# Unread products on TensorE ahead of a gather, one expert slot's products ahead of the fill tables, and scatters ahead of gathers on GpSimd

## What is computed

```python
probs = jax.nn.softmax(logits, axis=-1)
_, idx = jax.lax.top_k(probs, TOPK)
weights = probs * jax.nn.one_hot(idx, E, dtype=probs.dtype).sum(-2)
out = jnp.zeros_like(x)
for e in range(E):
    h = jax.nn.silu(x @ w1[e]) * (x @ w3[e])
    out = out + h @ w2[e] * weights[:, e:e + 1]
x = x + jnp.tanh(g_ffn[0]) * out
```

## Time and profile before

| | us |
|---|---|
| median of three runs | 699.2 |
| lowest and highest run | 697.81, 699.62 |
| profiled execution | 698.2 |
| its span, first to last instruction | 696.4 |
| TensorE busy | 638.3 (92%) |
| VectorE busy | 600.1 (86%) |
| ScalarE busy | 549.8 (79%) |
| GpSimd busy | 463.8 (67%) |

### The profile page before, as it was taken

One profiled execution on the slowest core, in us unless ns is written; L12 is line 12 of the kernel. 1 busy time (PEld: TensorE's weight loads), 2 busy tenths in 40 slices (PEclk: granted clock), 3 DMA queues, 4 the chain that ended last, 5 costly groups with the idle time before them and its releaser, 6 DMA issues. The chain is left out here.

```text
span 696.4 us, 14843 instructions
## 1 busy us (share of the span) xinstructions
PE 638.3 (92%) x4509; PEld 584.2 (84%) x4510; DVE 600.1 (86%) x1386; ACT 549.8 (79%) x1927; POOL 463.8 (67%) x646
## 2 busy tenths in 40 slices
PE   1579999999999999999999999999998479999994
PEld 0578899999999999999999999999977457888883
DVE  7797899999989999998999999888898877777771
ACT  5787889998998999999899999988875245666670
POOL 4777777688677768867786886787565425454532
PEclk9989999999999999999999999999999669999998
DMA  7101100020020102002000110200099412323232
GB/s 224 61 1 57 36 1 31 2 61 32 1 62 2 32 1 62 32 1 62 1 32 1 54 42 2 62 2 1 1 355 341 159 31 49 52 53 53 46 45 23
DMA packets 35509, 37.72 MB, mean 54 GB/s; under 512 B 2704, under 2 KB 30352, under 8 KB 35440
## 3 DMA queue, kind: packets, MB, share of 16 engines
q1 hardware_dynamic: 31024, 30.84, 13.3%
q0 software_dynamic: 4416, 6.03, 5.4%
HBM read 31.62 MB, written 5.24 MB: 53 GB/s over the span
## 5 line engine op out<-in xcount | busy, mean ns | idle before, releaser
L1459 POOL TENSOR_SCALAR shared<-shared,rsum 128x256 f32<-128x256 f32 x256 | 143.8, 573 | 56.1 <-DVE rsum L1004 51.0
L707 ACT ACTIVATE shared<-s,nmax 128x256 f32<-128x256 f32 x256 | 122.2, 498 | 22.9 <-DVE nmax L999 22.7
L1453 POOL TENSOR_TENSOR rstd<-rstd,half 128x7 f32<-128x7 f32 (+1 forms) x64 | 88.8, 1387 | 5.3
L999 DVE TENSOR_REDUCE nmax<-s 128x2 f32<-128x512 f32 x128 | 86.7, 680 | 3.1 <-PE s L380 3.0
L1009 DVE TENSOR_TENSOR pt_lo<-t,pt_hi 128x512 fp32r<-128x512 f32 x124 | 84.2, 679 | 1.9 <-ACT pt_hi L715 0.9
L715 ACT CAST pt_hi<-t 128x512 fp32r<-128x512 f32 x124 | 74.1, 597 | 9.8 <-PE t L395 7.2
L723 ACT ACTIVATE shared<-route_bank,head_w 128x512 f32<-128x512 f32 (+1 forms) x124 | 81.5, 689 | 0.0
L395 PE MATMUL t<-ident,shared 128*128 128x128 f32 x496 | 75.3, 275 | 5.9 <-POOL shared L1459 2.7
L994 DVE TENSOR_TENSOR qk_lo<-shared,qk_hi 128x512 fp32r<-128x512 f32 x96 | 78.3, 815 | 2.4 <-POOL qk_hi L1470 1.3
L336 PE MATMUL pj_a<-w_ring,xq 128*128 128x256 f32 x488 | 72.9, 293 | 6.9 <-POOL xq L1535 6.9
L2007 DVE TENSOR_TENSOR w_lo<-expert_w,w_hi 128x1024 fp32r<-128x1024 f32 x46 | 56.2, 1224 | 25.6 <-ACT w_hi L1885 24.9
(11 more groups left out here) (275 smaller groups left out, 1929.1 us busy)
## 6 DMA issues: line engine op xcount, KB each, us to landing
expert_w<-in_w SPq DMA_DIRECT2D x24, 512.0 KB, 9.2
spare<-in_wT SPq DMA_DIRECT2D x19, 256.0 KB, 3.1
wp_raw<-in_wpT SPq DMA_DIRECT2D x16, 256.0 KB, 2.9
spare<-in_wkvT SPq DMA_DIRECT2D x16, 128.0 KB, 3.3
spare<-in_wT SPq DMA_DIRECT2D x9, 128.0 KB, 3.6
spare<-in_x SPq DMA_DIRECT2D x1, 1024.0 KB, 5.9
x_hat<-acc SPq DMA_DIRECT2D x1, 1024.0 KB, 4.6
out<-spare SPq DMA_DIRECT2D x1, 1024.0 KB, 6.9
```

Of the source, the lines that this page charges most:

```text
L707: e = act.activation(probs[:, st, h * S:(h + 1) * S], s_bank[st][:, h * S:(h + 1) * S], ACT.Exp, bias=nmax[:, st, h:h + 1], accum_out=psum ...
L999: dve.tensor_reduce(nmax[:, st, :], s_bank[st][:].rearrange("p (h t) -> p h t", h=2), AX, ALU.max, negate=True).then_inc(max_done, 1)
L1453: pool.tensor_tensor(rstd[:, st, c], rstd[:, st, c], half[:, c], ALU.pow).then_inc(rstd_ready, 1)
L1459: m = pool.tensor_scalar(probs[:, st, c], probs[:, st, c], rsum[:, st, h:h + 1], 1.0, ALU.mult, ALU.mult)
```

## The change

Five edits in `experts`:

1. TensorE multiplies the identity by 128 columns of `acc` ten times ahead of its wait for `slots_known`, and twice more behind the transposes of slot 0. The products go to a bank that is written anew before it is read.
2. On TensorE the fill products go behind `down(0)`; `down(1)`, which writes over them, waits for `out_known`.
3. On VectorE the register load of slot 0's expert comes first, then the four operations up to `factor`, then the weight remainders of slot 0, then four of the operations that split `factor`, then the row split of slot 0 and `last_rows`, then the last of the nine.
4. On VectorE `take_hidden(0)` and the copy to `row_scale` come ahead of the fill tables, and `out_rows_known` goes into step 0, ahead of `take_y(0)`.
5. On GpSimd five gathers go ahead of the wait for `out_known` instead of four, and then scatter n goes ahead of gather n + 5.

```diff
@@ tensor
+            def stay_awake(times):
+                for _ in range(times):
+                    pe.matmul(h3_bank[1][:, 0:P], ident[:], acc[:, 0, 0:P], start=True, stop=True)
+
+            stay_awake(10)
             pe.wait_ge(slots_known, 1)
             turn_rows(0, 0)
+            stay_awake(2)
             hidden(0, 0, 0)
...
                 if isinstance(n, int) and n == 0:
-                    find_fill()
                     pe.wait_ge(scales_known, 1)
                     pe.wait_ge(tokens_known, 1)
+                if isinstance(n, int) and n == 1:
+                    pe.wait_ge(out_known, 1)
                 down(n, par)
+                if isinstance(n, int) and n == 0:
+                    find_fill()
@@ vector
-            (L1972 to L1984, the nine linked operations, ahead of the rest)
...
+                if isinstance(n, int) and n == 0:
+                    out_rows_known()
+                    dve.wait_ge(scales_known, 1)
                 take_y(n, par)
...
             e = expert_of(0)
+            (wait for exped and f_gated, L1974 to L1977)
             weights_rest(0, 0, e, 0)
             weights_rest(0, 0, e, 1)
+            (L1979 to L1983)
             rows_rest(0, 0)
             last_rows()
+            (L1984)
             slot_scales()
             e = expert_of(1)
             weights_rest(1, 1, e, 0)
             rows_rest(1, 1)
             weights_rest(1, 1, e, 1)
+            take_hidden(0, 0)
+            dve.wait_ge(scales_found, 1)
+            dve.tensor_copy(row_scale[:], y_bank[0][:, 0:SLOTS]).then_inc(scales_known, 1)
             fill_places()
             fill_table()
-            dve.wait_ge(scales_found, 1)
-            dve.tensor_copy(row_scale[:], y_bank[0][:, 0:SLOTS]).then_inc(scales_known, 1)
-            take_hidden(0, 0)
-            out_rows_known()
-            dve.wait_ge(scales_known, 1)
             steps(dve, step)
@@ gpsimd
-            for n in range(4):
+            for n in range(5):
                 load(n, n % 2)
             pool.wait_ge(route.sums_begun, 16)
             pool.wait_ge(out_known, 1)
             for n in range(SLOTS):
-                if n + 4 < SLOTS:
-                    load(n + 4, n % 2)
-                if n >= 1:
-                    scatter(n - 1, (n - 1) % 2)
-            scatter(SLOTS - 1, (SLOTS - 1) % 2)
+                scatter(n, n % 2)
+                if n + 5 < SLOTS:
+                    load(n + 5, (n + 1) % 2)
```

More of the change, by code:

```diff
@@ L1737, in experts @@
             sem("last_known"), sem("last_ranked"), sem("fill_known"), sem("fill_found"), sem("out_known"))
+        factored = sem("factored")
         weighed, scales_found, scales_known = sem("weighed"), sem("scales_found"), sem("scales_known")
@@ L1970, in _ @@
             dve.tensor_scalar(slot_expert[:], slot_f[:], float(E - 1), None, ALU.min).then_inc(slots_known, 1)
[L1972 to L1984, removed]
             def slot_scales():
@@ L2075, in _ @@
             e = expert_of(0)
+            dve.wait_ge(exped, 1)
+            dve.wait_ge(route.f_gated, 1)
+            link(dve.tensor_reduce(total[:], prob[:, :, 0:E], AX, ALU.add))
+            link(dve.reciprocal(total[:], total[:]))
+            link(dve.tensor_scalar(total[:], total[:], route.fgate[:, 0:1], None, ALU.mult))
+            dve.tensor_tensor(factor[:], prob[:, :, E:E + TOP].rearrange("p t j -> p j t"),
+                              total[:].rearrange("p (o t) -> p o t", o=1).broadcast_to([P, TOP, NT]), ALU.mult).then_inc(factored, 1)
             weights_rest(0, 0, e, 0)
             weights_rest(0, 0, e, 1)
+            dve.wait_ge(factored, 1)
+            whole = factor[:].rearrange("p j t -> p (j t)")
+            link(dve.tensor_copy(factor_part[:, 0, :], whole))
+            link(dve.tensor_tensor(left[:, 0, :], whole, factor_part[:, 0, :], ALU.subtract))
+            link(dve.tensor_copy(factor_part[:, 1, :], left[:, 0, :]))
+            dve.tensor_tensor(left[:, 1, :], left[:, 0, :], factor_part[:, 1, :], ALU.subtract).then_inc(factored, 1)
             rows_rest(0, 0)
             last_rows()
+            dve.wait_ge(factored, 2)
+            link(dve.tensor_copy(factor_part[:, 2, :], left[:, 1, :]))
             slot_scales()
```

## The result

The changed kernel takes 694.86 us (median of six runs, 693.82 to 695.21), the kernel before 698.47 (six runs, 697.76 to 699.62). The ratio is 0.9943, with a 95% interval of 0.9932 to 0.9954: 3.61 us less, where 3.7 were forecast (the forecast time, 695.5, was counted from a median of 699.2). The profiled execution of the changed kernel took 695.16, with a span of 693.3.

What follows compares the result with a forecast made beforehand. TensorE's steady state, 5.19 us per slot, sets the time, so starting it earlier gains: 2.57 from the clock and some 1.2 from the order, 3.7 off 699.2, giving 695.5 us; range 694.2 to 698.2.

Steps and rivals of the forecast that it cites:

- The clock: TensorE, products of slots 0 and 1: full clock from the first product on saves 2.57 us, bounds 0 and 2.57.
- The order: TensorE up to the transposes of slot 4: reordered work removes waits on VectorE, gaining some 1.2 us.
- The start: VectorE ahead of slot 0: the row split starts at 561.84 as before, 0 gained, bounds -0.25 and +0.25 us.
- The ten products: TensorE, while it waits for the gather: 0.53 us each, 5.3 in all, ending 0.8 behind the gather but covered.
- The rise: TensorE's clock rises after 3.0 to 5.4 us of work, at 558.6 to 561.0, ahead of slot 0's first product.
- `hid` early: VectorE: `hid` of slot 0 moves ahead of the fill tables, ending at 567.9 instead of starting at 570.20.
- `out_known` ahead of `down(1)`: TensorE's new wait: set at 574.7, `down(1)` reached at 575.7, so it costs nothing; cover 1.0 us.
- GpSimd's order: Five gathers ahead of `out_known`, then scatter 0 ahead of gather 5: costs nothing, bounds 0 and +1.4 us.
- The unmoved clock: Rival: the clock rises as late as before despite the unread products; gain only 1.2 us, 698.0; chance 0.16.
- The clock that falls back: Rival: the clock rises early but falls as slot 0's products begin, losing 1.28 us; gain 2.5, 696.7; chance 0.14.
- Gather 5 behind scatter 0: Rival: gather 5 moves rows only once scatter 0 has landed, 1.4 us late; gain 2.3, 696.9; chance 0.08.
- the slower rival: Rival: scatter rounds stay at 5.85 us against 5.19 per slot, making the kernel some 6 us slower, 705.5; chance 0.06.

Runs made afterwards that it cites:

- B: Kernel before plus only the unread products, ten ahead of the gather and five instead of two behind the transposes of slot 0: ratio 0.9993 to the kernel before.
- C: Changed kernel without the unread products, so only the new order: ratio 0.9965 to the kernel before, median 696.38 us.
- H: Changed kernel with VectorE's old start, all nine factor operations ahead of the register load: ratio 0.9969 to the kernel before.
- A: Kernel before plus only the twelve unread products, ten ahead of the gather and two behind the transposes of slot 0: ratio 0.9987 to the kernel before.
- J: Changed kernel with 24 instead of ten unread products ahead of the gather: ratio 0.9981 to the kernel before.
- E: Changed kernel with the fill products ahead of `down(0)` and `out_rows_known` ahead of the steps again: ratio 0.9961 to the kernel before.
- G: Changed kernel, still five gathers ahead of the wait for `out_known`, but then gather n + 5 ahead of scatter n: ratio 0.9932 to the kernel before.
- D: Changed kernel with `hid` of slot 0 and the copy of the scales behind the fill tables again: ratio 0.9982 to the kernel before.
- F: Changed kernel with GpSimd's old order, four gathers ahead of the wait for `out_known`: ratio 0.9979 to the kernel before.
- L: Changed kernel with five of the nine factor operations on GpSimd, between its second and third gathers: ratio 0.9923 to the kernel before, median 693.62 us.

## Why the prediction was right

The sum came out term by term. From the first product of slot 0 to the transposes of slot 4 it said 15.2, and the chain shows 15.20 (to the hundredth by chance: 0.1 of the 15.2 was for a wait that did not come, and the transposes of slots 1 to 3 took some 0.05 longer each than priced). The parts of the 4.08 are in the table's columns:

- **The clock, 2.57 forecast.** Between slot 0 and the transposes of slot 2 the changed kernel takes 11.16 - 6.75 = 4.41, the kernel before 14.04 - 7.11 = 6.93: 2.52. B, in which nothing else differs up to there, gives 2.53. (C puts it at 2.19, as the clock rose 0.6 sooner behind the first product there than in the kernel before.)
- **The order, some 1.2 forecast.** From the transposes of slot 2 to those of slot 4: 11.83 before, 10.63 after, 1.20. The 0.1 charged for the remainder of slot 2 was not needed; it ended at 573.08, before TensorE's products at 573.52.
- **The start, 0 forecast, bounds 0.25 either way.** This was the mis-sized term: 0.36, outside its bounds. The factor operations end at 559.93 and the remainders begin at 560.06 with no wait, 3.29 into the stage; in the kernel before they began 4.36 in. So the remainders come 1.07 earlier, where "about 1.0" was told. It is not the register load that left the path ahead of them, for it still costs 1.01 there, but the five operations that split `factor` (557.30 to 558.49 before). And the four operations ahead of the row split take 0.71 (562.34 to 563.05), where I had charged 1.0 by the spacing of linked operations; 1.07 - 0.71 is the 0.36. H confirms it from the other side, with 0.42. Beyond its size, H and A suggest that this edit also keeps the pause at 1.13 and so the clock up, which the prediction had priced as a rival and not tied to edit 3.

2.52 + 1.20 + 0.36 = 4.08. The medians differ by 3.61, so 0.47 of this is not in them, and no row here says why; that they meet the forecast 3.7 so closely is partly luck, as this and the 0.36 of the start nearly cancel. The changed kernel's later start of the stage (556.77 against 555.20) is not the work of the change's instructions, which all come behind it; the three executions of kernels without the order began at 555.20 to 555.64, the ten others at 554.78 to 557.74. Whether that is chance I cannot say.

The smaller steps, in their order. **The ten products** were priced at 0.53 for a pair, to end 0.8 behind the gather; they took 4.17 us, 0.42 a pair, and ended 0.36 ahead of it, so the cover of 0.7 was not touched. The cover itself was right to 0.01 (J). **The rise** was forecast 3.0 to 5.4 us after the first product of that stretch; it came after 3.5, and after 2.6 to 4.9 in the other executions (below 3.0 in E and G), always ahead of slot 0. **`hid` early** was needed as told, and its price without it is 2.17 (D); that without it the clock's gain would mostly vanish (B) is in none of the prediction's sentences, though its sum contains it. **`out_known` ahead of `down(1)`** costs nothing: VectorE has the last of the three operations at 575.15, and `down(1)` starts at 576.83, a cover of some 1.5 where 1.0 was forecast.

**GpSimd's order** was forecast to cost nothing, and does: the transposes of slot 5 start at 583.74 on TensorE's timeline, 5.18 behind those of slot 4, with no wait for gather 5. But "now goes at about 567.3" hid a price: `out_known` comes no earlier in the stage than before, so the sum needed gather 4 ahead of it, and without that 1.33 would have been lost (F). The right sentence would have been that the other edits need this one.

The rivals. The unmoved clock was priced at a gain of 1.2 (plus a start of 0); C, which leaves the products out, gains 1.87, of which 0.33 is the start and 0.33 the sooner rise. The clock that falls back is real (A, H), and costs 1.57 (H) rather than 1.28, since the transposes of slot 1 and part of the second six products of slot 0 run slow too. Gather 5 behind scatter 0 is refuted by the DMA rows: scatter 1, which waits for scatter 0 to land, was issued at 581.92, and by 581.6 the traffic of scatter 0 and gather 5 was over. The second of the two transfers moved its rows from 1.4 to 2.4 us behind the issue of gather 5 (579.20); gather 4, which had no scatter ahead of it, moved its rows from 1.6 to 2.3 behind its issue (570.2 to 570.9, after 568.62). So the scatter did not hold the gather. The rule of the Trainium skill that the prediction weighed (DMA: Bandwidth & Descriptors, section "SWDGE vs HWDGE vs iDMA": started in order, but pipelined) agrees with these rows. The scatter's rounds went from 5.30 (576.62 to 581.92) to 4.69 and 4.60, under the 5.19 of a slot, so the slower rival never came to its point.

## What to carry to other kernels

Cost the start of a steady stage as a race of two engines, and look in the row behind each gain for the wait that will eat it: here a clock worth 2.5 us alone kept 0.8, and an order worth 1.9 alone let it keep all. If an edit brings one engine forward, list every queue that feeds it and has not moved; the fifth gather was such a feed, and worth 1.33 us. Unread products are cheap while they end before the data that TensorE waits for, and cost one for one from where their cover ends; a dependent engine that is made ready sooner may matter as much for the pause that it leaves as for its own time (H).

## What the runs showed of the hardware

- The granted clock fell back from 1.00 to 0.50 in two of eleven executions with unread products, 0.4 to 0.5 us after the products of slot 0 had begun, behind a pause of 1.47 us; with pauses up to 1.13 it did not. The earlier trace rows had shown a fall within 2.39 us of idle time. The time from the first unread product to the rise varied from 2.6 to 4.9 us between executions of the same instructions.
- A gather can take longer than the median of 2.8 in the earlier trace rows: from the start of its issue to its landing the chain of F shows 3.77 us and that of L 3.93.
- Five elementwise operations of 128 x 16 took 0.20 to 1.07 us each on GpSimd, the first of either kind the longest (L: 0.41 and 0.20, 1.07 and 0.22), against 0.17 to 0.36 for the same five on VectorE ahead of the change.
